# A linear-attention input stage: token-order reads, the value bias and a subtraction moved to TensorE, copies moved to ScalarE

## The chip, the core and the metric

The kernel runs on one core of a Trainium2 chip. The core has TensorE (PE) for matrix products, with its own loader of the stationary operand (PEld), VectorE (DVE), ScalarE (ACT), GpSimd (POOL) and SyncE (SP), whose queue issues the transfers between memory and the on-chip buffer SBUF. Products land in PSUM. The metric is device time in microseconds for one execution.

## What is computed

Two transformer layers over 8 sequences of 1024 tokens with 256 features. The change touches one of seven phases, the first of layer 1: it adds up what layer 0's experts left, normalises it, adds it to the residual, normalises again and forms the features of a causal linear attention. Cut to that:

```python
# x: (8, 1024, 256); 16 heads of 16
x = x + _layernorm(ffn_output)                # ffn_output = shared + acc0 + acc1
qkv = _layernorm(x) @ W_qkv + b_qkv
q, k, v = jnp.split(qkv, 3, axis=-1)
q = jax.nn.elu(q * E ** (-0.5)) + EPS_FEAT    # EPS_FEAT = 1 + 1e-4
k = jax.nn.elu(k) + EPS_FEAT
```

The next phase reads q and k turned (feature on the partition, token along the row), k once more in token rows, and v in token rows with a column of ones behind every head.

## The kernel before

The seven phases stand one behind the other with a barrier between them. The phase in question is `phase_linear_qkv`, with the prefix `lqk` in the profile. The names below are its own.

It works on 16 blocks of 512 tokens, two for each sequence. A block lies as 4 tiles of 128 tokens, and partition p holds tokens 4p to 4p+3, so that tile t holds every fourth token. Every block goes through three stages, and `pipeline` runs them staggered: in one step, block n is in stage a, block n-1 in stage b and block n-2 in stage c. Each engine has its own program, which goes through its part of a, b and c in a fixed order written by hand, and waits on semaphores. There is no scheduler. Steps 2 to 15 run in a loop of two steps a turn.

- **Stage a.** GpSimd adds the three parts into `a0` (L1677, L1678). VectorE takes mean and variance (L745 to L750), GpSimd the power -1/2 (L1686), VectorE the shift (L756), ScalarE normalises into `yn` (L1781).
- **Stage b.** VectorE adds: `x2 = x1 + yn` (L1711), then mean and variance. GpSimd takes the power, VectorE the shift, ScalarE writes `xn` tile by tile (L1770). TensorE turns `xn` into `t_ps` (L1817, eight 128x128 transposes). ScalarE copies `t_ps` to `xh`, rounded to fp32r (L1787), and VectorE writes the rest `xl = t_ps - xh` (L1743). SP stores x2 and loads the inputs of the block after next.
- **Stage c.** TensorE forms q and k in four groups `qk[:, 0..3]`, each of six 128x512 products (high and low parts of weight and data, L738), and the value in `vp`, of 24 products of 128x256. ScalarE takes the exponential of each group (L1759), VectorE clips two groups at a time (L1727) and writes `phi` = max(qk + bias + 1, ex) for each (L1729). It also writes `vo = vp + bias` (L1735). TensorE turns the two k groups of `phi` back into `t_ps` (L1832, the "k turn") and ScalarE copies them to `kt` (L1791). SP stores vo, the two phi and kt.

Three orders matter. `t_ps` holds first the turned `xn`, then the turned k: the k turn waits for `xl` of stage b, and for all four `phi`. The next step's q and k products stand behind the k turn in TensorE's program. And SP is one queue: the loads of a step stand behind the stores of `kt` of the step before.

The columns of `qk` stand in the order of the tiles (column t*128+q is token 4q+t). L1729 puts them in token order, through the view

```python
        def in_order(a):
            return a.rearrange("p (t q) -> p q t", t=TPB)
```

in which two neighbouring elements lie 128 elements, or 512 bytes, apart.

Of the kernel before, what the change touches and what calls it, by code (L numbers as in the profile page):

```python
# [16 lines left out]
P = 128  # L17
# [1526 lines left out]
def phase_linear_qkv(nc, x1_d, sh_d, acc0_d, acc1_d, w_d, bqk_d, bv_d, x2_d, fq_d, fk_d, fkt_d, v_d):  # L1544
# [6 lines left out]
    with Phase(nc, "lqk") as ph:  # L1551
# [5 lines left out]
        bv = ph.sb("bv", [P, C])  # L1557
        ident = ph.sb("ident", [P, P])
        mhalf = ph.sb("mhalf", [P, TPB])
# [41 lines left out]
        xh_ready = ph.sem("xh_ready")  # L1601
        xl_ready = ph.sem("xl_ready")
# [6 lines left out]
        vo_ready = ph.sem("vo_ready")  # L1609
        x2_stored = [ph.sem(f"x2_stored{j}") for j in range(2)]  # L1610
# [18 lines left out]
        with nc.Block() as block:  # L1629
            @block.sync  # L1630
            def _(e):
# [6 lines left out]
                def stages(a, b, c):  # L1638
# [19 lines left out]
                e.dma_start(bv[:], bv_d.rearrange("(o n) -> o n", o=1).broadcast_to((P, C))).then_inc(w_loaded, 16)  # L1658
# [34 lines left out]
            def _(e):  # L1693
# [7 lines left out]
                split_weights(e, step, wf, wh, wl)  # L1701
                e.sem_inc(pe_consts, 1)
                e.wait_ge(ones_ready, 1)
                step.close()

                def stages(a, b, c):
# [16 lines left out]
                    if c is not None:  # L1723
                        j = c[1]
                        for half in (slice(0, 2), slice(2, 4)):
                            e.wait_ge(exp_ready, half.stop)
                            step(e.tensor_scalar(ex[:, half], ex[:, half], 1.0, FE, ALU.min, ALU.add))  # L1727
                            for k in range(half.start, half.stop):
                                e.scalar_tensor_tensor(phi[:, j, k].rearrange("p (q t) -> p q t", t=TPB),  # L1729
                                                       in_order(qk[:, k]), bqk1[:, k:k + 1], in_order(ex[:, k]),  # L1730
                                                       ALU.add, ALU.max).then_inc(phi_done, 1)
                        e.wait_ge(v_ready, 1)
                        for f in range(2):
                            cols = slice(f * P, (f + 1) * P)
                            i = e.tensor_tensor(vo[:, j, f].rearrange("p t (h d) -> p t h d", d=VW)[:, :, :, 0:HD],  # L1735
                                                vp[:, :, cols].rearrange("p t (h d) -> p t h d", d=HD),
                                                bv[:, cols].rearrange("p (h d) -> p h d", d=HD).unsqueeze(1)
                                                .broadcast_to((P, TPB, NH // 2, HD)), ALU.add)
# [12 lines left out]
            def _(e):  # L1751
                e.wait_ge(bias_ready, 1)
                for j in range(2):
                    e.sem_inc(x2_stored[j], 16)
                    e.sem_inc(stored[j], STORES)
# [1063 lines left out]
```

## Time and profile before

| | us |
|---|---|
| median of 3 runs | 3262.55 |
| the runs | 3261.11, 3262.55, 3276.6 |
| profiled execution | 3258.48 |
| its span | 3256.8 |
| the phase: first transfer to last k turn | 1662.4 to 1953.6 |
| PE busy / DVE busy / ACT busy, of the span | 87% / 68% / 49% |
| one step in the middle of the phase | 16.1 |

The shares of the span are means over seven phases with different limits. For this change only the stage between 1662 and 1960 counts, and in it the views of that stretch.

### The profile page before, as it was taken

The numbers are of one execution on the slowest core, as the hardware profiler recorded it, in microseconds if no ns is written. First come the engines' busy times: TensorE is split into PE (matmuls) and PEld (weight loads), VectorE is DVE, ScalarE is ACT, GpSimd is POOL, SyncE is SP. The second block draws the span as 40 slices with busy tenths as digits, with TensorE's granted clock in tenths as the row PEclk, the third lists the DMA queues.
The fourth block names the chain that finished last, engine by engine and source line by source line (L and its number), as shares of the span: only waits on it lengthen the run. The fifth ranks groups of instructions, "written<-read, shape, count | busy, mean of one in ns | idle before, by whom it ended". The sixth has DMA issues, their size and how long they took to land. (4 is left out here: it accounts for less than half of the span.)

```text
span 3256.8 us, 59136 instructions
## 1 busy us (share of the span) xinstructions
PE 2842.0 (87%) x20033; PEld 2062.9 (63%) x20033; DVE 2225.7 (68%) x6134; ACT 1603.0 (49%) x2446; POOL 731.5 (22%) x882
## 2 busy tenths in 40 slices
PE   7959999999999387689947777998399999999998
PEld 6834444444444276578836664555388888888887
DVE  6768999999997388663338883444466666666664
ACT  3506777777777244333325544544244444444443
POOL 1022222222222133247744422222000000000000
PEclk9959999999999666699968888999699999999999
DMA  6984556666662377648857867653432424243331
GB/s 244 330 153 83 108 115 112 112 112 116 112 110 65 127 270 269 214 138 225 221 165 269 296 228 228 183 162 100 132 99 74 122 65 117 78 102 92 90 86 46
DMA packets 342662, 485.87 MB, mean 149 GB/s; under 512 B 58832, under 2 KB 203248, under 8 KB 342384
## 3 DMA queue, kind: packets, MB, share of 16 engines
q1 hardware_dynamic: 331776, 468.94, 52.1%
q0 software_dynamic: 10240, 14.16, 2.3%
q8 instruction: 85, 1.39, 0.2%
q10 hardware_dynamic: 496, 0.84, 0.1%
q14 instruction: 65, 0.53, 0.1%
HBM read 278.77 MB, written 204.53 MB: 148 GB/s over the span
## 5 line engine op out<-in xcount | busy, mean ns | idle before, releaser
L551 ACT ACTIVATE att_pr<-att_e_ps 128x1024 f32<-128x1024 f32 (+2 forms) x640 | 567.3, 938 | 203.8 <-PE att_e_ps L603 203.8
L579 PE MATMUL att_m_ps<-att_ks,att_qs 63*128 63x512 f32 (+3 forms) x1536 | 465.9, 433 | 40.2 <-PEq L41 31.7
L513 DVE CUSTOM_DVE_ANT_0 att_kept<-att_m_ps,att_causal 128x256 f32<-128x256 f32 (+3 forms) x1024 | 448.5, 488 | 50.3 <-DVEq L41 21.9
L579 PEld LDWEIGHTS att_m_ps<-att_ks,att_qs 63*128 63x128 f32 x1536 | 234.3, 189 | 370.6 <-DVE att_mx L516 148.5
L492 POOL TENSOR_SCALAR_AFFINE_SELECT att_pr<-att_pr 128x256 f32<-128x256 f32 (+1 forms) x384 | 181.4, 485 | 698.0 <-PEq L594 694.5
L516 DVE TENSOR_REDUCE att_mx<-att_m_ps 128x1 f32<-128x512 f32 x512 | 323.3, 684 | 21.5 <-PE att_m_ps L579 17.5
L623 PE MATMUL att_o_ps<-att_pr,att_vs 128*32 128x512 f32 (+3 forms) x3072 | 328.7, 501 | 3.7 <-issue 2.0
L2604 ACT ACTIVATE fin_hh<-fin_hid 128x512 fp32r<-128x512 f32 x192 | 121.4, 632 | 399.8 <-DVE fin_hid L2450 302.2
L603 PE MATMUL att_e_ps<-att_qs,att_ks 64*128 64x512 f32 (+3 forms) x1536 | 269.1, 376 | 6.7 <-ACT att_pr L551 3.3
L2343 POOL TENSOR_TENSOR fin_rs<-fin_ve,fin_mhalf 128x4 f32<-128x4 f32 x48 | 48.4, 1007 | 928.6 <-POOLq L41 928.6
L2446 DVE TENSOR_TENSOR fin_hid<-fin_gate,fin_u_ps 128x512 f32<-128x512 f32 x192 | 131.5, 685 | 136.4 <-ACT fin_gate L2598 82.9
L738 PE MATMUL fin_f_ps<-fin_fhd,fin_hh 128*128 128x256 f32 x768 | 219.5, 286 | 0.2 <-DVE fin_hl L2465 0.2
L738 PE MATMUL fin_f_ps<-fin_fhd,fin_hl 128*128 128x256 f32 x768 | 216.3, 282 | 0.0
L738 PE MATMUL fin_f_ps<-fin_fld,fin_hh 128*128 128x256 f32 x768 | 216.2, 282 | 0.0
L2465 DVE TENSOR_TENSOR fin_hl<-fin_hid,fin_hh 128x512 fp32r<-128x512 f32 x192 | 132.5, 690 | 104.5 <-ACT fin_hh L2604 100.8
L1949 DVE TENSOR_TENSOR lin_am<-lin_a_ps,lin_tri 128x512 f32<-128x512 f32 x128 | 88.5, 692 | 143.5 <-PE lin_a_ps L2032 143.5
L603 PEld LDWEIGHTS att_e_ps<-att_qs,att_ks 64*128 64x128 f32 x1536 | 150.1, 187 | 38.8 <-ACT att_pr L551 13.5
L738 PE MATMUL fin_u_ps<-fin_xh,fin_fhu 128*128 128x512 f32 x384 | 153.0, 398 | 0.0
L738 PE MATMUL fin_g_ps<-fin_xh,fin_fhg 128*128 128x512 f32 x384 | 152.5, 397 | 0.0
L738 PE MATMUL fin_g_ps<-fin_xh,fin_flg 128*128 128x512 f32 x384 | 151.9, 396 | 0.0
L738 PE MATMUL fin_u_ps<-fin_xh,fin_flu 128*128 128x512 f32 x384 | 151.6, 395 | 0.0
L738 PE MATMUL fin_u_ps<-fin_xl,fin_fhu 128*128 128x512 f32 x384 | 151.5, 394 | 0.0
(332 smaller groups left out, 6921.2 us busy)
## 6 DMA issues: line engine op xcount, KB each, us to landing
fin_raw<-weights SPq DMA_DIRECT2D x32, 1024.0 KB, 9.6
att_qs<-q_high SPq DMA_DIRECT2D x128, 128.0 KB, 5.2
att_ks<-k_high SPq DMA_DIRECT2D x128, 128.0 KB, 6.5
attended<-att_ot SPq DMA_DIRECT2D x64, 256.0 KB, 8.5
acc<-att_zero SPq DMA_DIRECT2D x64, 256.0 KB, 2.2
moe_w<-w SPq DMA_DIRECT2D x128, 128.0 KB, 3.4
lqk_a<-acc SPq DMA_DIRECT2D x32, 512.0 KB, 6.0
attended<-lin_ot SPq DMA_DIRECT2D x32, 512.0 KB, 3.7
```

The lines of the kernel that those rows point to most:

```text
L492: e.affine_select(out=blk, in_=blk, compare_op=ALU.is_ge, fill=0.0, base=0, pattern=lead + [[1, P]], channel_multiplier=-1).then_inc(maske ...
L513: e.tensor_tensor_reduce(kept[:, n % MBUF, 0:w], m_ps[:, n % MBUF, 0:w], causal[:, BLK - w:], 1.0, -3e38, ALU.add, ALU.max, mx[:, h, at, q ...
L516: e.reduce_max(mx[:, h, at, q:q + 1], m_ps[:, n % MBUF, 0:w], AX.X).then_inc(m_free, 1)
L551: e.activation(out, src, ACT.Exp).then_inc(exp_done, 1)
L579: e.matmul(m_ps[:, (2 * i + n) % MBUF, 0:w], qs[rows, j, p, q * P:(q + 1) * P], ks[rows, j, p, h * BLK:h * BLK + w], start=True, stop=True ...
L603: i = e.matmul(e_ps[:, s % 2, n, m * w:(m + 1) * w], ks[rows, j, p, k * P:(k + 1) * P], qs[rows, j, p, (h + 1) * BLK - w:(h + 1) * BLK], s ...
L623: i = e.matmul(o_ps[32 * hd:32 * hd + 32, BLK - w:BLK], vs[:, j, k, hd * VW:hd * VW + 32], pr[:, u % NPR, hd // 2, hd % 2, 0:w], start=k = ...
L738: i = e.matmul(out, a, b, start=first and n == 0, stop=last and n == len(terms) - 1, **kw)
L1949: e.tensor_tensor(am[:, n % 2, 0:F // 2].rearrange("p (r h) q -> p r h q", h=2), a_ps[:, 0:2, 0:2 * P].rearrange("p r (h q) -> p r h q", h=2),
L2446: product_ = e.tensor_tensor(hid[:, c % 2], gate[:, c % 2], u_ps[:, c % 2], ALU.mult)
L2465: e.tensor_tensor(hl[:, c % 3], hid[:, c % 2], hh[:, c % 3].bitcast(fp32), ALU.subtract).then_inc(hl_ready, 1)
L2604: e.activation(hh[:, c % 3], hid[:, c % 2], ACT.Copy).then_inc(hh_ready, 1)
```

## The change

In the c stage the products of q and k read `xh` and `xl` through `in_order`, so that `qk` comes out in token order and L1729 reads and writes plain rows. The value bias is added by two products with one row of ones (bias in a high and a low part). The rest `t_ps - xh` is formed in PSUM, by a product of `xh` with minus the identity that adds onto `t_ps`. For that the turn of `xn` is a product with the identity that opens the accumulation, no longer a transpose. ScalarE copies the value out (`vo`) and the rest (`xl`).

```diff
-        bv = ph.sb("bv", [P, C])
+        bv = ph.sb("bv", [1, C])
+        bvh = ph.sb("bvh", [1, C], f32r)
+        bvl = ph.sb("bvl", [1, C], f32r)
+        one = ph.sb("one", [1, P], f32r)
+        minus = ph.sb("minus", [P, P], f32r)
...
@@ SP, stage c
                         e.wait_ge(vo_ready, 1)
+                        e.sem_inc(v_read, 1)
...
@@ DVE, before the first step
+                e.wait_ge(pe_consts, 1)
+                step(e.tensor_scalar(minus[:], ident[:], -1.0, None, ALU.mult))
+                split_weights(e, step, bv, bvh, bvl)
+                step(e.memset(onef[:], 1.0))
+                step(e.tensor_copy(one[:], onef[:]))
...
@@ DVE, stages
-                                e.scalar_tensor_tensor(phi[:, j, k].rearrange("p (q t) -> p q t", t=TPB),
-                                                       in_order(qk[:, k]), bqk1[:, k:k + 1], in_order(ex[:, k]),
-                                                       ALU.add, ALU.max).then_inc(phi_done, 1)
-                        e.wait_ge(v_ready, 1)
-                        for f in range(2):
-                            cols = slice(f * P, (f + 1) * P)
-                            i = e.tensor_tensor(vo[:, j, f].rearrange("p t (h d) -> p t h d", d=VW)[:, :, :, 0:HD],
-                                                vp[:, :, cols].rearrange("p t (h d) -> p t h d", d=HD),
...
-                    if b is not None:
-                        e.wait_ge(xh_ready, 1)
-                        e.tensor_tensor(xl[:, b[1]], t_ps[:], xh[:, b[1]].bitcast(fp32), ALU.subtract
-                                        ).then_inc(xl_ready, 1)
+                                e.scalar_tensor_tensor(phi[:, j, k], qk[:, k], bqk1[:, k:k + 1], ex[:, k], ALU.add,
+                                                       ALU.max).then_inc(phi_done, 1)
...
@@ ACT, stages, behind the copy to xh
+                        e.wait_ge(v_ready, 1)
+                        for f in range(2):
+                            cols = slice(f * P, (f + 1) * P)
+                            i = e.activation(vo[:, c[1], f].rearrange("p t (h d) -> p t h d", d=VW)[:, :, :, 0:HD],
+                                             vp[:, :, cols].rearrange("p t (h d) -> p t h d", d=HD), ACT.Copy)
+                        i.then_inc(vo_ready, 1)
+                    if b is not None:
+                        e.wait_ge(rest_ready, 1)
+                        e.activation(xl[:, b[1]], t_ps[:], ACT.Copy).then_inc(xl_ready, 1)
...
@@ PE, stages
-                                    (lambda k: xh[:, j, k], lambda k: xl[:, j, k]), KC).then_inc(qk_ready, 1)
+                                    (lambda k: in_order(xh[:, j, k]), lambda k: in_order(xl[:, j, k])), KC
+                                    ).then_inc(qk_ready, 1)
...
-                                i = e.transpose(t_ps[:, k, t * P:(t + 1) * P], xn[:, t, k * P:(k + 1) * P], ident[:])
+                                i = e.matmul(t_ps[:, k, t * P:(t + 1) * P], xn[:, t, k * P:(k + 1) * P], ident[:], start=t == 0,
+                                             stop=t == TPB - 1)
...
+                        e.wait_ge(v_read, 1)
...
+                            e.matmul(vp[:, t], one[:], bvh[:], start=False, stop=False)
+                            i = e.matmul(vp[:, t], one[:], bvl[:], start=False, stop=True)
...
+                    if b is not None:
+                        e.wait_ge(xh_ready, 1)
+                        for k in range(KC):
+                            i = e.matmul(t_ps[:, k], minus[:], xh[:, b[1], k], start=False, stop=True,
+                                         skip_group_check=True)
+                        i.then_inc(rest_ready, 1)
```

On TensorE, at the end of a step in the loop, where the last value products (`vp`), the k turn and the next step's first q and k products (`qk`) stand:

```order
 L738 MATMUL lqk_vp<-lqk_wl,lqk_xh 128x256
 L738 MATMUL lqk_vp<-lqk_wh,lqk_xl 128x256
-L1832 MATMUL lqk_t_ps<-lqk_ident,lqk_phi 128x128 x8
+L1839 MATMUL lqk_vp<-lqk_bvh,lqk_one 128x256
+L1840 MATMUL lqk_vp<-lqk_bvl,lqk_one 128x256
+L1846 MATMUL lqk_t_ps<-lqk_xh,lqk_minus 128x512 x2
+L1856 MATMUL lqk_t_ps<-lqk_ident,lqk_phi 128x128 x8
 L738 MATMUL lqk_qk<-lqk_xh,lqk_wh 128x512
 L738 MATMUL lqk_qk<-lqk_xl,lqk_wh 128x512
```

The k turn moves behind the two bias products of the fourth tile (the other three tiles have two each as well) and the two products that form the rest.

On ScalarE, one step of the loop before (`ex` exponential, `xn` and `yn` normalised tiles, `xh` and `kt` copies):

```order
L1759 ACTIVATE lqk_ex<-lqk_qk,lqk_bqk 128x512 x2
L1770 ACTIVATE lqk_xn<-lqk_x,lqk_nmr,lqk_rs 128x256 x4
L1759 ACTIVATE lqk_ex<-lqk_qk,lqk_bqk 128x512 x2
L1781 ACTIVATE lqk_yn<-lqk_a,lqk_nmr,lqk_rs 128x256 x4
L1787 ACTIVATE lqk_xh<-lqk_t_ps 128x1024
L1791 ACTIVATE lqk_kt<-lqk_t_ps 128x1024
```

The same step of the changed kernel:

```order
L1758 ACTIVATE lqk_ex<-lqk_qk,lqk_bqk 128x512 x2
L1769 ACTIVATE lqk_xn<-lqk_x,lqk_nmr,lqk_rs 128x256 x4
L1758 ACTIVATE lqk_ex<-lqk_qk,lqk_bqk 128x512 x2
L1780 ACTIVATE lqk_yn<-lqk_a,lqk_nmr,lqk_rs 128x256 x4
L1786 ACTIVATE lqk_xh<-lqk_t_ps 128x1024
L1792 ACTIVATE lqk_vo<-lqk_vp 128x32x16 x2
L1797 ACTIVATE lqk_xl<-lqk_t_ps 128x1024
L1801 ACTIVATE lqk_kt<-lqk_t_ps 128x1024
```

Three copies have come between the copy to `xh` and the copy to `kt`.

## Rows read from the trace of the kernel before

**Rows 1.** Groups of instructions, 1662 to 1974 us: busy us, mean ns, idle before.

```profile
L1729 DVE SCALAR_TENSOR_TENSOR lqk_phi<-lqk_qk,lqk_bqk,lqk_ex 128x512 f32<-128x512 f32 x64 | 69.4, 1127 | 1.1
L1735 DVE TENSOR_TENSOR lqk_vo<-lqk_vp,lqk_bv 128x512 f32<-128x512 f32 x32 | 20.5, 682 | 0.0
L1743 DVE TENSOR_TENSOR lqk_xl<-lqk_t_ps,lqk_xh 128x1024 fp32r<-128x1024 f32 x16 | 19.4, 1215 | 3.9 <-ACT lqk_xh L1787 3.9
```

**Rows 2.** Waits, 1695 to 1940 us: total, times, longest us.

```profile
PE lqk_t_ps L1832 <- DVE lqk_xl L1743: 51.2, 14, 5.4
```

**Rows 3.** Timeline of VectorE over one step: start, duration us.

```profile
1796.77 2.31 DVE L1711 TENSOR_TENSOR lqk_x<-lqk_x,lqk_yn 128x1024 f32<-128x1024 f32 x1
...
1801.47 1.41 DVE L745 BATCH_NORM_STATS2 lqk_st<-lqk_a 128x6 f32<-128x256 f32 x4
...
1804.78 0.16 DVE L756 SCALAR_TENSOR_TENSOR lqk_nmr<-lqk_mv,lqk_rs 128x4 f32<-128x4 f32 x1 [0.98 <-POOL lqk_rs L1686]
...
1808.48 2.12 DVE L1729 SCALAR_TENSOR_TENSOR lqk_phi<-lqk_qk,lqk_bqk,lqk_ex 128x512 f32<-128x512 f32 x2
1810.52 1.28 DVE L1735 TENSOR_TENSOR lqk_vo<-lqk_vp,lqk_bv 128x512 f32<-128x512 f32 x2
...
1812.85 2.29 DVE L1711 TENSOR_TENSOR lqk_x<-lqk_x,lqk_yn 128x1024 f32<-128x1024 f32 x1
```

**Rows 4.** Timeline of TensorE: the pace of its kinds of product.

```profile
1504.39 1.03 PE L1530 MATMUL moe_eh_ps<-moe_xt,moe_w 128*128 128x96 f32 x8
1505.21 0.47 PE L738 MATMUL moe_h_ps<-moe_xh,moe_w1h 128*128 128x512 f32 x1
...
1725.43 0.39 PE L738 MATMUL lqk_qk<-lqk_xh,lqk_wl 128*128 128x512 f32 x1
1725.66 1.03 PE L1817 MATMUL lqk_t_ps<-lqk_ident,lqk_xn 128*128 128x128 f32 x8
...
1726.65 0.28 PE L738 MATMUL lqk_vp<-lqk_wl,lqk_xh 128*128 128x256 f32 x1
...
1727.48 0.28 PE L738 MATMUL lqk_vp<-lqk_wh,lqk_xl 128*128 128x256 f32 x1
...
1812.99 1.24 PE L1832 MATMUL lqk_t_ps<-lqk_ident,lqk_phi 128*128 128x128 f32 x8 [3.76 <-DVE lqk_xl L1743]
...
1815.37 0.63 PE L738 MATMUL lqk_qk<-lqk_xl,lqk_wh 128*128 128x512 f32 x1
1815.80 0.63 PE L738 MATMUL lqk_qk<-lqk_xh,lqk_wl 128*128 128x512 f32 x1
```

**Rows 5.** Weight loads that write `t_ps`: ns min/median/max, first and last start.

```profile
L1817 PEld LDWEIGHTS lqk_t_ps<-lqk_ident,lqk_xn x128: 137/141/226, 1692.3 to 1934.8; 128*128 128x128 f32 x128
L1832 PEld LDWEIGHTS lqk_t_ps<-lqk_ident,lqk_phi x128: 195/218/231, 1716.4 to 1953.6; 128*128 128x128 f32 x128
```

**Rows 6.** Reads of the first phase's `qkv_qk`, ns min/median/max.

```profile
L243 ACT ACTIVATE qkv_oh<-qkv_qk x64: 595/598/602, 21.5 to 165.3; 128x512 fp32r<-128x512 f32 x64
L216 DVE TENSOR_TENSOR qkv_ol<-qkv_qk,qkv_oh x64: 675/682/692, 22.9 to 165.9; 128x512 fp32r<-128x512 f32 x64
```

**Rows 7.** Timeline of ScalarE over the same step.

```profile
1798.61 1.02 ACT L1791 ACTIVATE lqk_kt<-lqk_t_ps 128x1024 f32<-128x1024 f32 x1 [4.76 <-PE lqk_t_ps L1832]
...
1803.83 2.08 ACT L1770 ACTIVATE lqk_xn<-lqk_x,lqk_nmr,lqk_rs 128x256 f32<-128x256 f32 x4 [0.63 <-DVE lqk_nmr L756]
...
1808.93 1.01 ACT L1787 ACTIVATE lqk_xh<-lqk_t_ps 128x1024 fp32r<-128x1024 f32 x1
1814.26 1.02 ACT L1791 ACTIVATE lqk_kt<-lqk_t_ps 128x1024 f32<-128x1024 f32 x1 [4.32 <-PE lqk_t_ps L1832]
```

**Rows 8.** Timeline of GpSimd: the second of its two additions.

```profile
1814.13 3.23 POOL L1678 TENSOR_TENSOR lqk_a<-lqk_a 128x1024 f32<-128x1024 f32 x1
```

**Rows 9.** All instances of that addition, ns min/median/max.

```profile
L1678 POOL TENSOR_TENSOR lqk_a<-lqk_a x16: 2337/3242/3260, 1675.3 to 1911.0; 128x1024 f32<-128x1024 f32 x16
```

**Rows 10.** Stretch behind one k turn: PE busy, PEclk.

```profile
1797.50:1800.90 3.40, 3.40 (x12) 0.50 0.28 108
```

More of the change, by code:

```diff
@@ L1556, in phase_linear_qkv @@
         bqk1 = ph.sb("bqk1", [P, 4])
-        bv = ph.sb("bv", [P, C])
+        bv = ph.sb("bv", [1, C])
+        bvh = ph.sb("bvh", [1, C], f32r)
+        bvl = ph.sb("bvl", [1, C], f32r)
+        onef = ph.sb("onef", [1, P])
+        one = ph.sb("one", [1, P], f32r)
         ident = ph.sb("ident", [P, P])
+        minus = ph.sb("minus", [P, P], f32r)
         mhalf = ph.sb("mhalf", [P, TPB])
@@ L1601, in phase_linear_qkv @@
         xh_ready = ph.sem("xh_ready")
+        rest_ready = ph.sem("rest_ready")
         xl_ready = ph.sem("xl_ready")
@@ L1609, in phase_linear_qkv @@
         vo_ready = ph.sem("vo_ready")
+        v_read = ph.sem("v_read")
         x2_stored = [ph.sem(f"x2_stored{j}") for j in range(2)]
@@ L1657, in _ @@
                 e.dma_start(bqk[:], bqk_d).then_inc(w_loaded, 16)
-                e.dma_start(bv[:], bv_d.rearrange("(o n) -> o n", o=1).broadcast_to((P, C))).then_inc(w_loaded, 16)
+                e.dma_start(bv[:], bv_d.rearrange("(o n) -> o n", o=1)).then_inc(w_loaded, 16)
                 for j in range(2):
@@ L1701, in _ @@
                 split_weights(e, step, wf, wh, wl)
+                e.wait_ge(pe_consts, 1)
[3 more added lines that the diff above has]
+                step(e.tensor_copy(one[:], onef[:]))
                 e.sem_inc(pe_consts, 1)
-                e.wait_ge(ones_ready, 1)
                 step.close()
@@ L1728, in stages @@
                             for k in range(half.start, half.stop):
[L1729 to L1745 removed]
+                                e.scalar_tensor_tensor(phi[:, j, k], qk[:, k], bqk1[:, k:k + 1], ex[:, k], ALU.add,
+                                                       ALU.max).then_inc(phi_done, 1)
+                        take(e, (exp_ready, 4))
                     step.close()
@@ L1752, in _ @@
                 e.wait_ge(bias_ready, 1)
+                e.wait_ge(ones_ready, 1)
                 for j in range(2):
@@ L1789, in stages @@
                     if c is not None:
+                        e.wait_ge(v_ready, 1)
[7 more added lines that the diff above has]
+                        e.activation(xl[:, b[1]], t_ps[:], ACT.Copy).then_inc(xl_ready, 1)
+                        take(e, (rest_ready, 1))
+                    if c is not None:
                         e.wait_ge(k_turned, 1)
@@ L1792, in stages @@
                                      ).then_inc(kt_ready, 1)
-                        take(e, (qk_ready, 4), (k_turned, 1))
+                        take(e, (qk_ready, 4), (v_ready, 1), (k_turned, 1))
                 pipeline(e, stages, 3)
@@ L1802, in _ @@
                 e.wait_ge(pe_consts, 2)
+                e.sem_inc(v_read, 1)
                 def stages(a, b, c):
@@ L1820, in stages @@
                     if c is not None:
+                        e.wait_ge(v_read, 1)
                         for t in range(TPB):
                             cols = slice(t * P, (t + 1) * P)
-                            i = product(e, vp[:, t], (lambda k: xh[:, j, k, cols], lambda k: xl[:, j, k, cols]),
-                                        (lambda k: wh[:, k, 2 * C:3 * C], lambda k: wl[:, k, 2 * C:3 * C]), KC)
+                            product(e, vp[:, t], (lambda k: xh[:, j, k, cols], lambda k: xl[:, j, k, cols]),
+                                    (lambda k: wh[:, k, 2 * C:3 * C], lambda k: wl[:, k, 2 * C:3 * C]), KC, last=False)
+                            e.matmul(vp[:, t], one[:], bvh[:], start=False, stop=False)
+                            i = e.matmul(vp[:, t], one[:], bvl[:], start=False, stop=True)
                         i.then_inc(v_ready, 1)
+                        take(e, (v_read, 1))
+                    if b is not None:
[4 more added lines that the diff above has]
+                        i.then_inc(rest_ready, 1)
+                        take(e, (xh_ready, 1))
                     if c is not None:
```

3 lines of the change are left out of this document (removed).

## The prediction

> **What bounds the kernel now.** The shares of the whole span say nothing here, so I first read the groups of the stretch from 1662 to 1974 us, then who waits there, then one step of each engine in order of time.
>
> Between the sum `x2` of one step and that of the next VectorE runs without a gap but for 0.98 us for GpSimd's power: 1796.77 to 1812.85, a step of 16.08 us [rows 3]. There is little idle time ahead of its groups [rows 1]. TensorE does wait, 51.2 us over 14 steps, for `xl` [rows 2], 3.7 us a step. So VectorE sets the pace.
>
> A second chain is nearly as long. A step's loads stand in SP's queue behind the stores of the last `kt`, so from the end of a copy to `kt` (1798.61 + 1.02 = 1799.63, [rows 7]) it takes until 1814.13 + 3.23 = 1817.36 [rows 8] before GpSimd's sum is there: 17.73 us. The statistics of the sum start 0.15 us later (VectorE's at 1801.47 are the same place one step back, [rows 3]), and from their start to the end of that step's `kt` it is 13.81 us (1815.28 less 1801.47, [rows 3, 7]). Together 31.7 us for two steps, 15.85 each. Relieving VectorE alone can thus give little unless this chain shortens too.
>
> **The change part by part.** Every step is told as a time in the c stage; there are 16 such steps. In the trace the first k turn starts at 1716.4 and the last at 1953.6 less seven transposes, 1952.7 [rows 5]: 236.3 us for 15 intervals.
>
> *VectorE.* Gone are `vo`, 1.20 us a step (1810.52 to 1811.72, its two overlap by a little, [rows 3]), and `xl`, 1.13 (to 1812.85). L1729 keeps its four instructions. It takes 1127 ns for 512 elements [rows 1]. In the first phase a VectorE instruction reads `qkv_qk` through the same order and an SBUF operand in plain order in 682 ns [rows 6], so the 445 ns are the price of `ex`, read from SBUF at 512 bytes apart. In plain order I take 0.68, a gain of 1.8 us a step. VectorE falls from 16.08 to about 12.0 us. It bounds no longer.
>
> *TensorE, the new products.* A transpose follows the next every 0.108 us: (1.03 - 0.27)/7 [rows 4]. A plain product of fp32 operands does not run as one: the eight records of moe_eh_ps stand for four products, and take (1505.21 - 1504.39)/8 = 0.11 each with overlap at the end, so 0.23 us for one [rows 4]. Eight of them: 1.84 us instead of 0.87. Value products follow at (1727.48 - 1726.65)/7 = 0.119 us [rows 4], 24 of them plus 8 for the bias 3.80 us. The two that form the rest take as long as a q or k product, 0.234 (1725.43 to 1725.66), 0.47 together. Before, a step's wait for `xl` hid such work; now these stand in the chain below.
>
> *TensorE, the reads in token order.* 24 products a step read 512 columns at 512 bytes apart. No row shows a moving operand that is read so. Four rows stand near. A plain one takes 0.234 us at the high level of the clock (0.43 at the low one, 1815.37 to 1815.80, [rows 4]), which bounds it from below: nothing in the change makes a read quicker than in plain order. The weight load of the k turn reads `phi` 16 bytes apart, and a median load grows from 141 to 218 ns [rows 5]; the whole turn takes 1.24 us against 1.03 [rows 4], of which about 0.1 is its first gap, so 0.12 us for 128 elements against 0.108. That is 0.945 ns an element, at a pace at which a plain load needs 0.85, and a plain moving read 0.234/512 = 0.46. If a read far apart goes at 0.945 ns, a product takes 0.484 us; if at 0.85, the pace of plain loads, 0.43. VectorE's operand pays 0.87 ns an element more (445/512): 0.68 us a product, and at most 1127/512 = 2.2 ns, 1.13 us. I take the middle of the two TensorE prices, 0.455, since it is TensorE's own read, and keep 0.234 and 0.68 as ends. The row of VectorE says that the distance costs something in SBUF; the load says that TensorE feels it already at half the pace that these products need.
>
> The Trainium skill, SBUF — State Buffer, Specifications, bears on this: a line of SBUF has 16 bytes and wants at least two hits for full bandwidth. By it every element of these reads opens a line of its own, and half the pace would be an estimate of 0.43 us a product. That speaks against the change, and the weight load agrees in sign.
>
> *ScalarE.* Two copies of the value at 0.598 us [rows 6], 1.17 with their overlap, and the rest at 1.01, as `xh` [rows 7]. Its rows of a step add up to some 9 us before and 11 after. It does not bound by its sum, but it stands in the chain, since the k turn waits for the rest.
>
> *The chain of TensorE.* From the start of one step's q and k products to the next: 24 products at s, turn of `xn` 1.84, values and bias 3.80, 0.2 until ScalarE sees it, two copies 1.17, the rest 1.01, 0.1, and the k turn 0.97. That is 24 s + 9.1. The copy to `xh` and the two rest products fit beside the values and add at most 0.47. With s = 0.455 a step takes 20.0 us; with 0.43 it is 19.4, with 0.484 20.7. At s = 0.29 it is 16.1, as before: that is the point from which it decides.
>
> *New waits.* TensorE waits for `v_read` ahead of its values; SP gives it as soon as it has seen `vo`, a whole set of q and k products earlier, so it costs nothing unless SP is still at its loads. ScalarE waits for the values with the rest, `kt` and the next exponentials queued behind it, and then for the rest: both waits are in the chain above. SP's queue has the same transfers; only the bias comes in one row.
>
> *Once.* Before the first step VectorE makes `minus` and the bias parts, some 1.3 us, in time in which it waits for GpSimd's first sum. In step 1 the rest goes over TensorE to ScalarE: +0.5. The first c step I take 0.5 longer too.
>
> *Sum.* 14 intervals of 20.0 and the last of 15.7 (10.9 + 3.8 + 1.0, with no stage b) are 295.7 against 236.3: +59.4; with the two items of 0.5, +60. The profiled execution took 3258.48 us, 4 us less than the median of 3262.55. Against the median: 3322.
>
> **The rivals.**
>
> *The distance is free to TensorE (0.34).* For it: its load in the low state of the clock, and in the high one, shows a median rise but only 0.01 us a transpose in pace [rows 4, 5]; that may be a fixed charge. Then s = 0.234 and TensorE's chain takes 14.7 us. The second chain decides. GpSimd's addition takes 2.34 instead of 3.24 us [rows 9] when VectorE's `x2` no longer runs beside it, and it doesn't, since `x2` starts 3 us earlier relative to it: 17.73 - 0.90 = 16.83. From the statistics: `xh` ends after 8.5 us (1809.94 less 1801.47, [rows 3, 7]), the values after 8.7, two copies 9.9, rest 10.9, and from the k turn's start to the end of `kt` 2.3 (1812.99 to 1815.28, [rows 4, 7]) 13.2. Two steps in 16.83 + 0.15 + 13.2 = 30.2, so 15.1 each. 14 of these and a last of 10.4 are 221.8: -14.5, 3248 us, between -8 and -21. This is the case on the other side: the same mechanism with s under 0.29.
>
> *A small fixed charge (0.07).* With 0.01 to 0.05 us a product more, s lies between 0.245 and 0.29, a step takes 15.1 to 16.1 us: 3248 to 3262.
>
> *VectorE's price (0.07).* s = 0.68 gives 25.4 us a step, +140: 3402. With 1.13 it is 36 us, 3565.
>
> *The clock (0.03).* TensorE ran at 0.50 of its clock for 3.4 us behind each wait for `xl` [rows 10]. With less waiting I expect the high level throughout. If slow reads kept it low, values, turns and bias would take twice as long, some 6 us a step more than forecast: near 3410.
>
> The forecast itself gets 0.49.
>
> **How the numbers follow.** A measurement of this kernel can tell a change of about 0.5%, 16 us. The forecast, s from 0.43 to 0.484 and some slack, gives 3308 to 3340. The range reaches to the free case, of which it leaves out the last microseconds: 3243 to 3340. Outside it are VectorE's price, the clock and little else, about 0.15. Faster by over 0.5% is only the better part of the free case, 0.14. Within 0.5%: the rest of it and the small charge, 0.27. Slower: the forecast, VectorE's price and the clock, 0.59.
>
> **What would show it.** Right: the q and k products follow each other every 0.43 to 0.48 us at a granted clock of 1.0, L1741 (the former L1729) near 0.68 us, VectorE idle for 7 us a step, mostly in wait of ScalarE's exponentials, TensorE nearly without a wait but for some 2.5 us before the k turn, which ends on the rest (L1797). Steps of 20 us. Wrong: products that still follow every 0.234 us; then steps of 15.1, with VectorE waiting for GpSimd's sum ahead of its statistics. The turn of `xn` should show 16 records a step for 8 products. If L1741 stays near 1.1 us, the price was not that of the distance in `ex`, and VectorE's step is 13.8, still under both chains.

## The result, and the profile after

| | before | after |
|---|---|---|
| median us (runs beside each other) | 3261.39 (10) | 3276.72 (10) |
| lowest, highest | 3252.99, 3276.6 | 3263.13, 3290.6 |
| profiled execution | 3258.48 | 3284.51 |

The change makes the kernel slower: 1.0049 times the time of before, interval 1.0031 to 1.0067, or +15 us where +60 was forecast. It is at the edge of the 0.5% that a measurement of this kernel tells apart, though the interval leaves out 1. It lies inside the range of 3243 to 3340.

The views are those of before. First the group that was to get shorter (busy us, mean ns, idle before):

```profile
L1741 DVE SCALAR_TENSOR_TENSOR lqk_phi<-lqk_qk,lqk_bqk,lqk_ex 128x512 f32<-128x512 f32 x64 | 45.1, 746 | 1.1
```

L1741 is the L1729 of [rows 1]: 1127 ns have become 746. Then who waits, in the stretch of [rows 2]:

```profile
DVE lqk_st L745 <- POOL lqk_a L1686: 58.3, 12, 5.0
...
PE lqk_t_ps L1856 <- ACT lqk_xl L1797: 20.0, 14, 1.4
```

VectorE, which had no gap in a step but the 0.98 us for GpSimd's power [rows 3], now waits 58.3/12 = 4.86 us a step for GpSimd's sum. TensorE waits 1.43 us instead of 3.7, for ScalarE's copy of the rest. One step of TensorE, from k turn to k turn (start, duration us):

```profile
1813.00 1.23 PE L1856 MATMUL lqk_t_ps<-lqk_ident,lqk_phi 128*128 128x128 f32 x8 [1.43 <-ACT lqk_xl L1797]
1813.98 0.52 PE L738 MATMUL lqk_qk<-lqk_xh,lqk_wh 128*128 128x512 f32 x1
...
1819.41 0.45 PE L738 MATMUL lqk_qk<-lqk_xl,lqk_wh 128*128 128x512 f32 x1
1819.69 0.45 PE L738 MATMUL lqk_qk<-lqk_xh,lqk_wl 128*128 128x512 f32 x1
...
1820.83 1.95 PE L1829 MATMUL lqk_t_ps<-lqk_ident,lqk_xn 128*128 128x128 f32 x16
1822.53 0.36 PE L738 MATMUL lqk_vp<-lqk_wh,lqk_xh 128*128 128x256 f32 x1
...
1823.21 0.28 PE L738 MATMUL lqk_vp<-lqk_wh,lqk_xl 128*128 128x256 f32 x1
1823.41 0.38 PE L1839 MATMUL lqk_vp<-lqk_bvh,lqk_one 1*128 1x256 f32 x1
1823.63 0.28 PE L1840 MATMUL lqk_vp<-lqk_bvl,lqk_one 1*128 1x256 f32 x1
1823.84 0.38 PE L738 MATMUL lqk_vp<-lqk_wh,lqk_xh 128*128 128x256 f32 x1
1824.06 0.28 PE L738 MATMUL lqk_vp<-lqk_wl,lqk_xh 128*128 128x256 f32 x1
...
1827.84 0.73 PE L1846 MATMUL lqk_t_ps<-lqk_xh,lqk_minus 128*128 128x512 f32 x2
1830.00 1.23 PE L1856 MATMUL lqk_t_ps<-lqk_ident,lqk_phi 128*128 128x128 f32 x8 [1.43 <-ACT lqk_xl L1797]
```

The step is 17.00 us, and all 14 of the loop are 17.00 or 17.01. It adds up as follows. The q and k products follow each other at 0.28 us, 6.85 for the 24. The turn of `xn` shows its 16 records and takes 1.70. The values with their bias take 5.31: around the two bias products of a tile, whose operands have a single row, four starts in a row come 0.20 to 0.23 us behind the one before, instead of 0.12 (the first bias product, the second, and the two value products behind them). From the first product of the rest (L1846) to the k turn it is 2.16, the time of ScalarE's copies, and the k turn 0.98. Together 17.0.

The same step as a window (length; busy and count of PE, PEld, DVE, ACT, POOL; then PEclk, DMA share, GB/s):

```profile
1813.00:1830.00 17.00, 15.57 (x82) 11.89 (x82) 9.51 (x27) 10.50 (x17) 6.80 (x5) 1.00 0.76 280
```

The clock stays at 2.4 GHz (PEclk 1.00), where before it fell in each step, for 3.4 us in the one of [rows 10].

From the first k turn (1710.96) to the last (1962.11) it is 251.2 us against 236.3 before: +14.8, close to the 15.3 by which the medians differ. The profiled executions differ by 26. The next phase, whose code is the same, holds 15.9 more in them, first before:

```profile
1962.30:2267.70 305.40, 279.55 (x3808) 169.59 (x3808) 127.06 (x258) 148.56 (x256) 82.37 (x133) 0.92 0.54 167
```

and after:

```profile
1971.50:2292.80 321.30, 295.72 (x3808) 177.26 (x3808) 127.14 (x258) 148.77 (x256) 82.19 (x133) 0.87 0.51 158
```

with TensorE at a lower mean clock. In the sixteen profiles of the experiments this phase took 298 to 325 us, with a kernel of token-order reads at either end (e8 and e1), and the experts' phase ahead 291 to 303. So these two move from one execution to the next, and the steps of the changed phase are compared below, beside the medians. "Phase" in the table below is the time from the first to the last instruction that names one of its tiles.

### The profile page after: what moved, and what is told of

It reads as the page before. It is cut to its first block and busy times, and to the rows that moved or that the text cites. A ratio compares the mean times of both kernels' runs of the same rounds, so it can differ in the third digit from the quotient of the medians.

```text
span 3282.8 us, 59766 instructions
## 1 busy us (share of the span) xinstructions
PE 2912.2 (89%) x20321; PEld 2097.0 (64%) x20321; DVE 2155.8 (66%) x6091; ACT 1636.0 (50%) x2494; POOL 722.0 (22%) x882
## 3 DMA queue, kind: packets, MB, share of 16 engines
q8 instruction: 83, 1.36, 0.2%
## 5 line engine op out<-in xcount | busy, mean ns | idle before, releaser
L603 PEld LDWEIGHTS att_e_ps<-att_qs,att_ks 64*128 64x128 f32 x1536 | 150.5, 188 | 38.4 <-ACT att_pr L551 14.7
```

Of the source, the lines that this page charges most:

```text
L603: i = e.matmul(e_ps[:, s % 2, n, m * w:(m + 1) * w], ks[rows, j, p, k * P:(k + 1) * P], qs[rows, j, p, (h + 1) * BLK - w:(h + 1) * BLK], s ...
```

## The experiments

### Which part of the change costs what

No bias products (the value bias is left out of the output):

```diff
-                            e.matmul(vp[:, t], one[:], bvh[:], start=False, stop=False)
-                            i = e.matmul(vp[:, t], one[:], bvl[:], start=False, stop=True)
```

> The changed kernel without the two bias products of each tile (the value bias is left out). Theory: TensorE's own chain sets the step of 17.0 us, and the eight bias products, whose stationary operand has one row, cost 2.5 us of it where I had forecast 0.95 (the values and bias take 5.31 us, the 24 value products alone 24 x 0.118 = 2.8). Then TensorE's chain falls to 14.5 us and the chain over SP's loads and GpSimd takes over: step 14.9. Rival: the step is set already by that second chain (VectorE waits 4.9 us a step for GpSimd's sum), then it stays at 17.0. Second rival: the bias products cost what I had forecast, 0.95: step 16.0.

The changed kernel with q and k read in plain order and `phi` reordered by VectorE as before:

```diff
-                                    (lambda k: in_order(xh[:, j, k]), lambda k: in_order(xl[:, j, k])), KC
+                                    (lambda k: xh[:, j, k], lambda k: xl[:, j, k]), KC).then_inc(qk_ready, 1)
```

> The changed kernel with q and k products that read in the order of the tiles, and VectorE writing phi through the strided view as before. Theory: a product follows the next every 0.234 us again, not 0.283, so 24 of them give back 1.2 us: step 15.8, some 18 us less than the changed kernel's 3277, near 3259. VectorE's L1741 back at 1.13 us costs nothing, since VectorE waits (its own sum is 13.5 us). Rival: the second chain sets the step: 17.0, no difference. Rival: VectorE's four slower instructions lie on the way to the k turn: 17.0 or more.

The bias products with 128 rows, of which the first is one and the others nought, and the same with plain reads as well:

```diff
-        bv = ph.sb("bv", [1, C])
+        bv = ph.sb("bv", [P, C])
-        one = ph.sb("one", [1, P], f32r)
+        one = ph.sb("one", [P, P], f32r)
...
+                step(e.memset(onef[0:1], 1.0))
```

> The changed kernel with bias products over all 128 rows (a stationary operand that is one in row 0 and zero elsewhere), same sums. Theory: the price of the bias products lies in the change from 128 rows to one row and back (0.2 us ahead of each of the products around them), so with 128 rows they follow at 0.119 us like the value products: 3.8 us for values and bias instead of 5.3, step 15.5, time near 3254. Rival: the price lies in the operand shared by all or in the fp32r split, then nothing changes: 17.0.

> Both: plain reads and bias products over 128 rows. Theory: TensorE's chain is 14.3 us, the chain over SP and GpSimd (16.8 us from the end of one copy to kt to the sum, 12.9 from there to the end of the copy after next, 29.8 for two steps) sets 14.9: time near 3246, faster than before by 0.5%. Rival: the two prices don't add: 15.5 or more.

The kernel before with only the token-order reads and the plain `phi`:

> The kernel before with only the token-order reads: TensorE reads x in token order, VectorE's phi is plain, the value bias and the low half stay on VectorE. VectorE loses 4 x 0.38 = 1.5 us a step. Theory, that VectorE set the step before (16.1) and the chain over SP and GpSimd lies close behind: VectorE's run falls to 14.6, the second chain to 15 to 15.5, so steps of 15.0 to 15.6 with TensorE waiting less for the low half (its own work is 24 x 0.283 + 0.9 + 2.9 + 1.0 = 11.6 at the high clock), 3241 to 3249 us. Rival, that the longer products lie on the path and eat it: xl waits come later, and the step stays near 16.1, within 3 us of before.

| kernel | steps, us | phase, us | median us | against before |
|---|---|---|---|---|
| before | 15.35 to 16.66, the last 14.72 | 294.8 | | |
| after | 17.00 | 309.5 | 3276.72 | 1.0049 (1.0031 to 1.0067) |
| e1, no bias | 14.7 to 15.1, three of 15.8 | 276.5 | 3260.07, one run | |
| e2, plain reads | 15.86 once, then 17.06 | 308.8 | 3273.14 | 1.0061 (1.0042 to 1.0081) |
| e3, bias of 128 rows | 15.64 | 288.7 | 3261.58 | 1.0009 (0.999 to 1.0028) |
| e4, both | 14.49 to 15.67, mean 15.20 | 280.7 | 3242.93 | 0.9962 (0.9948 to 0.9976) |
| e8, token order alone | 14.56 to 15.95, the last 14.02 | 283.5 | 3249.17 | 0.9965 (0.9946 to 0.9983) |

The bias costs what its single row costs. With 128 rows, which is more data, the same eight products follow at the pace of their neighbours (TensorE of e3):

```profile
1800.49 0.28 PE L1840 MATMUL lqk_vp<-lqk_bvh,lqk_one 128*128 128x256 f32 x1
1800.61 0.28 PE L1841 MATMUL lqk_vp<-lqk_bvl,lqk_one 128*128 128x256 f32 x1
1800.73 0.28 PE L738 MATMUL lqk_vp<-lqk_wh,lqk_xh 128*128 128x256 f32 x1
```

and the step is 17.00 - 15.64 = 1.36 us shorter. That is more than the 1.0 us a step (14.8 over 15) that the change had lost against before.

Plain reads (e2) should have given 1.2 us a step, and gave them once: the first step is 15.86. From then on the clock fell around every k turn. The window of one step and that of its low stretch:

```profile
1806.65:1823.72 17.07, 15.64 (x83) 12.93 (x83) 12.94 (x28) 10.39 (x17) 6.71 (x5) 0.90 0.76 278
1806.10:1809.50 3.40, 2.85 (x11) 2.66 (x12) 0.96 (x1) 1.33 (x2) 3.32 (x3) 0.51 0.43 164
```

The k turn of that step takes 1.64 us (1808.29 less 1806.65) instead of 0.98 and the first products 0.43 instead of 0.23:

```profile
1806.65 1.98 PE L1856 MATMUL lqk_t_ps<-lqk_ident,lqk_phi 128*128 128x128 f32 x8 [1.43 <-ACT lqk_xl L1798]
1808.29 0.78 PE L738 MATMUL lqk_qk<-lqk_xh,lqk_wh 128*128 128x512 f32 x1
1808.86 0.63 PE L738 MATMUL lqk_qk<-lqk_xl,lqk_wh 128*128 128x512 f32 x1
1809.29 0.52 PE L738 MATMUL lqk_qk<-lqk_xh,lqk_wl 128*128 128x512 f32 x1
```

The 1.2 us won by the reads went to the clock. The wait ahead of the k turn is 1.43 us here as in the changed kernel, where the clock did not fall, so the rows do not say why it falls in one and not in the other. In e1, with token-order reads, it fell in three steps, which took a microsecond more than their neighbours (two neighbours of e1):

```profile
1802.03:1817.13 15.10, 13.48 (x75) 10.60 (x75) 10.89 (x28) 10.36 (x17) 7.37 (x5) 1.00 0.87 320
1817.13:1832.99 15.86, 14.24 (x74) 11.56 (x75) 11.12 (x33) 11.78 (x18) 7.08 (x5) 0.89 0.82 300
```

And e8 turns the forecast of the reads round: alone in the kernel before, the token-order reads are a gain of 0.35%, small, but with 1 outside the interval. They cost TensorE at most 24 x 0.05 = 1.2 us of time in which it waited, and save VectorE 4 x 0.38 = 1.5 us of the time that set the pace.

### What a read in another order costs

The price per product was the term on which the forecast rested. Seven kernels give it for other orders: the changed kernel with another view in the place of `in_order`, in all four q and k products, or one in each.

```diff
-                                    (lambda k: in_order(xh[:, j, k]), lambda k: in_order(xl[:, j, k])), KC
+                                    (lambda k: spread(xh[:, j, k]), lambda k: spread(xl[:, j, k])), KC
```

e5 has `"p (q t) -> p t q", t=4`, e6 the same with `t=2`, e7 `"p (t q u) -> p q t u", t=4, u=2`.

> The changed kernel with the moving reads of the q and k products 16 bytes apart instead of 512 (t = 4 in place of 128; the columns of a block come in another order, so its output has tokens exchanged). Theory, that a read pays for each 16 bytes that it opens: 0.28 us a product as with 512 bytes, steps of 17.0. Rival, that the distance of 512 bytes is what costs: 0.234 us a product, steps of 15.8 at the high clock, or 17.0 with the clock falling in each step as in the run with plain reads. Rival, a fixed charge per instruction that isn't read in plain order: 0.28 here too, told apart by the next two.

> As the last one, with the reads 8 bytes apart, so that two elements of every four lie in each 16 bytes. Theory (a charge for each 16 bytes opened): half of the charge, 0.26 us a product, if it is proportional; 0.234 if two elements of 16 bytes are enough to hide it. Rival (a fixed charge of an instruction): 0.28. Rival (distance of 512 bytes alone): 0.234.

> The changed kernel with the q and k reads 512 bytes apart in pairs: two neighbouring elements, then 512 bytes on (output has tokens exchanged). Theory (a charge for each 16 bytes opened): as with 8 bytes, 0.26 or 0.234 us a product. Rival (a charge for the distance or for the form of the access): 0.28, or more, since the read has one dimension more.

> The changed kernel with another order of reading in each of the four q and k products of a step (six instructions each; tokens of the output are exchanged): product 0 runs of 2 elements 1024 bytes apart, product 1 runs of 8 elements 256 bytes apart, product 2 runs of 4 elements 64 bytes apart, product 3 runs of 4 elements 512 bytes apart of which the next run begins 16 bytes on (in the change it begins 4 bytes on). Theory A, that four consecutive elements are read each by a path of its own that keeps its last 16 bytes: product 0 0.45 us an instruction, since each path alternates between two places, product 1 0.45 too, product 2 0.28, product 3 0.45. Theory B, that the reader keeps several recent lines of 16 bytes, whatever the order: products 0, 1 and 2 0.28 or less, product 3 0.45. Theory C, that only the length of the innermost run counts (4 is cheap, else dear): products 2 and 3 0.28, 0 and 1 0.45. Theory D, that elements 512 bytes apart lie in different banks and nearer ones collide: product 0 and 3 0.28, product 2 0.45.

> The same with product 0 runs of 16 elements 128 bytes apart, product 1 runs of 32 elements 64 bytes apart (the next run 4 bytes on), product 2 four neighbours (16 bytes) and then 512 bytes on, product 3 as the change (0.28). Theory A (a path for each of four consecutive elements, keeping 16 bytes): product 0 and 1 0.45, product 2 0.234 to 0.28. Theory B (several recent lines kept): product 0 0.28 if 16 lines are kept, product 1 0.28 if 32 are, product 2 0.234. Theory C (length of the innermost run): 0 and 1 0.45, product 2 0.234 to 0.28.

> As the two runs with four orders of reading each (tokens of the output exchanged): product 0 runs of 4 elements 512 bytes apart, the next run 8 bytes on; product 1 runs of 2 elements 1024 bytes apart, the next run 8 bytes on; product 2 runs of 4 elements 16 bytes apart, the next 4 bytes on; product 3 runs of 8 elements 8 bytes apart, the next 4 bytes on. Theory E (the reader keeps the 16-byte lines that the last four elements touched; an order that opens every line once is cheap, one that opens it twice or four times costs double): 0.45, 0.45, 0.27, 0.45 us. Theory F (a charge for each group of four elements that opens new lines, none for the others): 0.34, 0.45, 0.27, 0.34. Theory G (what counts is only that the innermost run has 4 or 2 elements that a next run finds within 8 bytes): 0.28, 0.22, 0.27, 0.45.

> Four new orders of reading, one in each q and k product (tokens of the output exchanged). Theory H (even and odd elements have a path each; a path keeps its last two lines of 16 bytes; one element out of each opened line halves the pace): product 0, runs of 2 elements 1024 bytes apart, the next run 16 bytes on, each path gets one element of a line: 0.45 us. Product 1, 2 neighbours, then 2 neighbours 1024 bytes on, then back: each path alternates between two lines and gets two elements of each: 0.34, as 4 elements 512 bytes apart with the next run 8 bytes on. Product 2, 4 neighbours, 4 neighbours 1024 bytes on, back to the next 16: two in a row of each line: 0.23 to 0.27. Product 3, runs of 2 elements 16 bytes apart, the next run 4 bytes on: four in a row of each line: 0.22. Rival K (only an element that follows its predecessor by 4 bytes, or an innermost run of 2 single elements, is cheap): product 0 0.23, product 1 0.45 as the pairs with four places, product 2 0.27, product 3 0.22.

16 bytes apart (e5), two products that follow each other, at 0.46 us:

```profile
1810.33 0.64 PE L738 MATMUL lqk_qk<-lqk_xh,lqk_wh 128*128 128x512 f32 x1
1810.79 0.64 PE L738 MATMUL lqk_qk<-lqk_xl,lqk_wh 128*128 128x512 f32 x1
```

The four orders of e9, one product after the other (TensorE):

```profile
1800.06 0.38 PE L738 MATMUL lqk_qk<-lqk_xh,lqk_wh 128*128 128x512 f32 x1
...
1800.71 0.72 PE L738 MATMUL lqk_qk<-lqk_xh,lqk_wh 128*128 128x512 f32 x1
...
1802.74 0.70 PE L738 MATMUL lqk_qk<-lqk_xl,lqk_wh 128*128 128x512 f32 x1
1803.23 0.70 PE L738 MATMUL lqk_qk<-lqk_xh,lqk_wl 128*128 128x512 f32 x1
...
1804.84 0.44 PE L738 MATMUL lqk_qk<-lqk_xl,lqk_wh 128*128 128x512 f32 x1
1805.11 0.44 PE L738 MATMUL lqk_qk<-lqk_xh,lqk_wl 128*128 128x512 f32 x1
...
1806.81 0.67 PE L738 MATMUL lqk_qk<-lqk_xh,lqk_wh 128*128 128x512 f32 x1
1807.29 0.67 PE L738 MATMUL lqk_qk<-lqk_xl,lqk_wh 128*128 128x512 f32 x1
```

In turn: three products from 1800.06 to 1800.71, 0.217 each; 0.49 to 0.52; 0.27; 0.48. The table has all orders, each as the distance of starts in rows like these (second to sixth product of six, by four; of the first order of e9 the three from 1800.06 on, where the granted clock is 1.00), sorted by what the last theory, H, counts. H deals the elements of a read to two paths in turn, in the order in which they are read: the first, third and fifth to one, the second, fourth and sixth to the other. A path keeps the last two lines of 16 bytes that it has read from. The last column has the number of elements that a path finds one after the other in a line.

| order of the elements | us a product | run | in a path and line |
|---|---|---|---|
| 2 places 16 B apart, next 4 B on | 0.215 | f4 | 4 in a row |
| 2 places 1024 B apart, next 4 B on | 0.217 | e9 | 4 in a row |
| plain | 0.233 | e2 | 2 in a row |
| 2 places 1024 B apart, next 8 B on | 0.233 | f1 | 2 in a row |
| 4 neighbours at each of 2 places, 1024 B | 0.25 | f4 | 2 in a row |
| 4 neighbours at each of 4 places, 512 B | 0.27 | e10 | 2 in a row |
| 4 places 16 B or 64 B apart, next 4 B on | 0.27 | f1, e9 | two lines in turn, 4 of each |
| **4 places 512 B apart, next 4 B on (the change)** | 0.283 | after, e10 | two lines in turn, 4 of each |
| 4 places 512 B apart, next 8 B on | 0.336 | f1 | two lines in turn, 2 of each |
| 2 neighbours at each of 2 places, 1024 B | 0.33 | f4 | two lines in turn, 2 of each |
| 16 places 128 B, 32 places 64 B apart | 0.434 | e10 | 1 |
| 2 neighbours at each of 4 places, 512 B | 0.446 | e7 | 1 |
| 2 places 1024 B apart, next 16 B on | 0.452 | f4 | 1 |
| every second element (8 B) | 0.453 | e6 | 1 |
| every fourth element (16 B) | 0.461 | e5 | 1 |
| 8 places 8 B apart, next 4 B on | 0.48 | f1 | 1 |
| 4 places 512 B apart, next 16 B on | 0.484 | e9 | 1 |
| 8 places 256 B apart, next 4 B on | 0.50 | e9 | 1 |

Distance says little: 8 bytes cost double, and 1024 bytes nothing. Of the theories A to D none fits e9 and e10; A fails on places 1024 bytes apart, D on 64, B on 8 places, C on the next run 16 bytes on. E, F and G each fail in f1, where the first product came out at 0.336, the second at 0.233, and the fourth at 0.48. Theory H was then made to fit the sixteen orders known by then, and put to four new orders. It gave 0.45, 0.34, 0.23 to 0.27 and 0.22; measured were 0.452, 0.33, 0.25 and 0.215. Its rival K fell in the first two (0.23 and 0.45). The four orders of f4 (TensorE; all but the first at PEclk 1.00, the first from 1805.69 to 1807.06 at 0.91):

```profile
1806.15 0.63 PE L738 MATMUL lqk_qk<-lqk_xl,lqk_wh 128*128 128x512 f32 x1
1806.60 0.63 PE L738 MATMUL lqk_qk<-lqk_xh,lqk_wl 128*128 128x512 f32 x1
...
1808.37 0.50 PE L738 MATMUL lqk_qk<-lqk_xl,lqk_wh 128*128 128x512 f32 x1
1808.70 0.50 PE L738 MATMUL lqk_qk<-lqk_xh,lqk_wl 128*128 128x512 f32 x1
...
1810.03 0.41 PE L738 MATMUL lqk_qk<-lqk_xl,lqk_wh 128*128 128x512 f32 x1
1810.27 0.42 PE L738 MATMUL lqk_qk<-lqk_xh,lqk_wl 128*128 128x512 f32 x1
...
1811.40 0.38 PE L738 MATMUL lqk_qk<-lqk_xl,lqk_wh 128*128 128x512 f32 x1
1811.61 0.38 PE L738 MATMUL lqk_qk<-lqk_xh,lqk_wl 128*128 128x512 f32 x1
```

H is a model that gives the numbers, and no more: that there are two paths and two lines for each is inferred from paces alone. Nor does it give all of them: it has no reason why the orders with one element to a line spread from 0.434 to 0.50, or why 0.25 and 0.27 stand beside 0.233.

One reading says where the time of the dear orders is not spent. They don't slow down with TensorE's clock: e7's products follow each other at 0.450 us where the granted clock is 0.50 (1759.15 to 1760.95) and at 0.447 where it is 1.00. A plain product in the kernel before takes 0.427 and 0.233, and one in the order of the change, in e8, 0.427 (behind the k turn at 1783.83) and 0.283. So at the low clock the token order costs nothing.

The Trainium skill, SBUF — State Buffer, Specifications, wants at least two hits in a line of 16 bytes for full bandwidth. Every second element has two in each line, one behind the other, and runs at half pace (0.453). The rule fits these runs only if the hits of the two paths of H are counted apart.

### Which chain sets the step behind the change

SP issues the stores of `phi` and `kt` one step later, behind the next step's loads:

```diff
+                    if late is not None:
+                        j = late[1]
+                        e.wait_ge(kt_ready, 1)
...
+                        e.dma_start(kt_v[late[0], j], kt[:, j].rearrange("p f t c -> p f (t c)")).then_inc(stored[j], 16)
...
-                pipeline(e, stages, 3, peeled=1)
+                pipeline(e, stages, 4, peeled=1)
```

> The changed kernel with the bias products of 128 rows (steps of 15.64 us in its run), and in it SP issues the stores of phi and kt one step later, behind the next step's loads, so that GpSimd's sum no longer waits for the last kt. Theory, that TensorE's own chain sets these steps: 15.6 us again, 3261 us, with VectorE waiting less for GpSimd. Rival, that the chain over SP and GpSimd sets them: steps of 15.0 or less.

> The kernel with plain reads and bias products of 128 rows (steps of 14.5 to 15.7, mean 15.2) with the same change in SP's queue. Theory, that there the chain over SP and GpSimd (two steps in 30.2) is what decides: steps fall to TensorE's own chain, 24 x 0.236 + 1.7 + 3.1 + 2.2 + 1.0 = 13.7 to 14.3 us, 3228 to 3233 us. Rival, that the step is TensorE's and varies with its clock: 15.2 us again, 3243 us.

> The kernel before with SP's stores of phi and kt one step later, behind the next step's loads; nothing else is changed. Theory, that VectorE's own run of 16.1 us sets its steps: 16.0 to 16.1, within 3 us of before. Rival, that the chain over SP and GpSimd (15.85) sets them as much: steps of 15.5 or less, at least 8 us faster.

> The kernel before with only the token-order reads (steps of 14.6 to 15.9, mean 15.4), and SP's stores of phi and kt one step later. Theory, that VectorE's run of 14.6 is what is left when the chain over SP and GpSimd is cut: steps of 14.6, 3238 us. Rival, that the low stretches of TensorE's clock after its wait for the low half are in the path: 15.2 to 15.4 as before, 3249 us.

e11 keeps its steps of 15.64 (0.9996, interval 0.9974 to 1.0018): there TensorE's own chain sets them, and with it those of 17.00 of the change, which differ by the bias products alone.

e12 has steps of 14.48 or 14.49 throughout, where e4 had 15.20 in the mean, and takes 0.9932 of the time of before (0.9905 to 0.9958), 3235.47 us in four executions. It has the lowest median of all. The wait of VectorE in e4:

```profile
DVE lqk_st L745 <- POOL lqk_a L1686: 29.3, 12, 2.5
```

has gone in e12:

```profile
DVE lqk_st L745 <- POOL lqk_a L1689: 2.4, 1, 2.4
```

So the second chain of the prediction exists, and decides once TensorE's is shorter than 15 us. The step that is left is TensorE's, 0.2 above the upper end of what was expected.

In the kernel before the same edit (f2) gives nothing: 1.001 (0.9994 to 1.0026), steps of 15.04 to 17.19. f3, with token-order reads, has 0.9982 (0.9963 to 1.0), no better than e8's 0.9965. Two neighbouring steps of f3:

```profile
1803.91:1818.13 14.22, 11.71 (x64) 9.27 (x64) 12.20 (x31) 8.50 (x14) 6.80 (x5) 1.00 0.93 328
1818.13:1834.62 16.49, 12.86 (x65) 10.40 (x65) 14.41 (x31) 9.79 (x15) 7.63 (x5) 0.85 0.85 299
```

Of the 2.27 us between them, 2.05 stand in one instruction, VectorE's clip of two groups (`ex`, L1730). It takes 0.68 us when it starts ahead of GpSimd's first addition, and lasts beyond the end of that addition when it starts just behind its start. Here are clip and addition in a step of f2 of 15.15 us, in its next of 17.19, and in the f3 step of 16.49:

```profile
1736.06 0.68 DVE L1730 TENSOR_SCALAR lqk_ex<-lqk_ex 128x1024 f32<-128x1024 f32 x1
1736.70 2.40 POOL L1680 TENSOR_TENSOR lqk_a<-lqk_a 128x1024 f32<-128x1024 f32 x1 [3.64 <-DMA lqk_a<-shared]
...
1751.29 2.73 DVE L1730 TENSOR_SCALAR lqk_ex<-lqk_ex 128x1024 f32<-128x1024 f32 x1
1751.07 2.40 POOL L1680 TENSOR_TENSOR lqk_a<-lqk_a 128x1024 f32<-128x1024 f32 x1 [2.79 <-DMA lqk_a<-shared]
...
1828.05 2.74 DVE L1730 TENSOR_SCALAR lqk_ex<-lqk_ex 128x1024 f32<-128x1024 f32 x1 [0.34 <-ACT lqk_ex L1761]
1827.84 2.40 POOL L1680 TENSOR_TENSOR lqk_a<-lqk_a 128x1024 f32<-128x1024 f32 x1 [2.43 <-DMA lqk_a<-shared]
```

So cutting the second chain lets GpSimd start earlier, and its additions move from beside `x2`, which they lengthen in the kernel before (2.31 us in the step of [rows 3], 1.21 at the shortest), to beside the clip. Take off each of the first 13 steps what `x2` and the clip last above their shortest, and what VectorE waits apart from the power. What is left is 14.9 to 15.4 us before and in f2, and 13.6 to 13.8 in e8 and f3. That is VectorE's own run, and it sets the steps of all four. The rest varies with what runs beside GpSimd's additions.

The rival of f3, the low stretches of the clock, has a smaller part. In the step of 16.49 VectorE waits 0.34 us for an exponential, which puts the clip behind the start of the addition; in the step of 17.19 of f2 it comes to lie there without such a wait. In the step behind it in f3 (16.19 us, clock 0.82) VectorE waits 1.65 us for exponentials, and the clip is only 0.85 too long. That these waits come from the low clock is likely, since the q and k products ahead of them run at it, but no run separates the two.

## Why the prediction was wrong in its size

**What bounds the kernel before.** VectorE's run, as the prediction said. e8 (VectorE relieved by 1.5 us a step, phase 11.3 us shorter) and f2 (second chain cut, no gain, and VectorE still without a wait but the power's in nearly every step) agree. The second chain, 15.85 us, was no floor: e8, which leaves it alone, has steps of 15.3 in the mean. And the prediction took `x2` at 2.3 us for a fixed length, where it is 1.2 and the time beside GpSimd's addition.

**The turn of `xn`, VectorE's price, the once-only items.** The 16 records took 1.70 against a forecast of 1.84, L1741 746 ns against 0.68 us. The last interval was 13.07, 4 us under the 17.0 of the loop as foreseen (20.0 and 15.7).

**Who waits.** TensorE's wait ahead of the k turn ends on the rest, as foreseen (1.43 us). VectorE's 7 us of idle time were to be "mostly in wait of ScalarE's exponentials"; they are mostly the wait for GpSimd's sum, 4.86 us, which the prediction had as a sign of the free case.

**The form of the sum.** TensorE's chain, 24 s + 9.1, was the right one: with the measured pace it gives 24 x 0.283 + 9.1 = 15.9, and with the bias at its true price 17.4, against 17.0 (the turn was 0.14 shorter and the stretch of the copies 0.3). The point from which it decides, 0.29, fits too: e3, at 0.283 and without the price of the single row, has steps of 15.64 and is equal to before in time (1.0009).

**The step that failed** is this one: "I take the middle of the two TensorE prices, 0.455, since it is TensorE's own read". The measured pace is 0.283, 24 x 0.172 = 4.1 us a step less. The row it came from, the weight load 16 bytes apart [rows 5], was no bad witness for its own order: a moving read 16 bytes apart costs 0.46 (e5). But the change reads in another one. After four elements its next run begins 4 bytes on, in the same 16 bytes, and no order measured whose next run begins 4 bytes on after two or four elements costs more than 0.283. The prediction saw the distance and left out what is read next.

**A term too small** was the bias: "24 of them plus 8 for the bias 3.80 us" priced a product with one row as one with 128. It measured 5.31, and e3 gives the difference back (1.36 a step, 20 us over the phase by steps; the ratios of after and e3, each against its own before, differ by 0.0040, or 13 us, with intervals of about 6 on each side). The two errors had opposite signs. With the pace right and the bias as forecast, the prediction would have been no change.

**The clock.** "I expect the high level throughout" held for the change, with its reasoning (less waiting keeps it up) not confirmed: e2 waits as little and lost the clock in every step but the first. With plain reads, the case of the first rival, e2 has 17.06 where the rival had 15.1: 1.2 us went to the clock, and the single row costs more than the 0.4 us that TensorE's chain was to lie under the second one. With the bias of 128 rows (e4) the steps are 15.20 in the mean, with VectorE waiting for GpSimd's sum, as that rival said.

## What to carry to other kernels

Price a strided read by the whole order, not by its distance: write down which 16 bytes each of the next eight elements lies in, and look for a row with that same pattern. A small product put between large ones isn't priced by its size; give it the shape of its neighbours. And when a gain on TensorE doesn't arrive, look at the granted clock of one step before looking for a new wait. When an edit moves GpSimd's additions in time, look at which of VectorE's instructions they now run beside.

## What the runs showed of the hardware

- A product of 512 fp32r columns takes 0.215 to 0.50 us by the order of its moving read alone, at a granted clock of 1.00; places 1024 bytes apart were faster (0.217) than plain order (0.233).
- The dear orders keep their pace when the clock falls: 0.450 us at a granted clock of 0.50 against 0.447 at 1.00 (e7), where a plain product takes 0.427 against 0.233.
- Two products with one row between products with 128 rows: four starts in a row 0.20 to 0.23 us apart where 0.12 is usual, gone when both operands have 128 rows (e3).
- VectorE's L1729 takes 1127 ns for 512 elements with both its reads (`qk` in PSUM, `ex` in SBUF) 512 bytes apart, and 746 with both plain. Another instruction with only the PSUM read in that order takes 682 [rows 6]. TensorE pays a fifth more for the same order.
- GpSimd's addition takes 2.36 us (median) instead of 3.24 [rows 9] once VectorE's `x2` no longer runs beside it, and `x2` 1.22 instead of 2.34. VectorE's clip takes 2.73 us instead of 0.68 when it starts 0.22 us behind GpSimd's addition (f2).
